# Attention with the weighted sums of two units ago laid between the scores in sixteenths, and own scores that contract over 32 rows

## What is computed

```python
q = _conv1x1(wq, x).reshape(n, NH, HD, H, W)          # n=4, NH=16 heads, HD=16, H=W=128
k = _conv1x1(wk, x).reshape(n, NH, HD, H, W)
v = _conv1x1(wv, x).reshape(n, NH, HD, H, W)
qk = jnp.einsum('nhcij,nhciw->nhijw', q, k) / D
qrq = jnp.einsum('nhcij,chjw->nhijw', q, rq) / D
krk = jnp.einsum('nhcij,chjw->nhijw', k, rk) / D
weight = jax.nn.softmax(qk + Gq * qrq + Gk * krk, axis=3)
out = jnp.einsum('nhijw,nhciw->nhcij', weight, Gv1 * v) + jnp.einsum('nhijw,chjw->nhcij', weight, Gv2 * rv)
return _conv1x1(wo, out.reshape(n, C, H, W))
```

## Time and profile before

| | us |
|---|---|
| median of 3 executions | 8304.97 |
| lowest and highest of them | 8296.95, 8308.47 |
| profiled execution: device time | 8291.75 |
| profiled execution: span from first to last instruction | 8290.0 |
| attention, from its first matmul to its last (1525.8 to 6664) | 5138.2 |
| mean granted TensorE clock, share of 2.4 GHz: whole span | 0.749 |
| the same in attention alone | 0.68 |

### The profile page before, as it was taken

How to read it: one execution, slowest core, us unless ns; L and a number is a source line. 1 busy time by engine, 2 the same in 40 slices (tenths; PEclk the granted TensorE clock), 3 DMA queues, 4 the chain that set the end, 5 groups by cost and what they waited for, 6 DMA issues and landing times. The chain is left out here.

```text
span 8290.0 us, 275612 instructions
## 1 busy us (share of the span) xinstructions
PE 7187.2 (87%) x106442; PEld 6044.4 (73%) x106442; DVE 5176.6 (62%) x20646; ACT 4856.3 (59%) x11427; POOL 2457.0 (30%) x1235
## 2 busy tenths in 40 slices
PE   4999999799999999999999899999999966766738
PEld 3555555689988888898899898898888932332338
DVE  5444444366666666666666666666666768988830
ACT  1444444577777777777777777777777733333410
POOL 0000000243443443444434444434434432322210
PEclk7999999666666666666666666666667688988855
DMA  7555555565655665655556656656656576766522
GB/s 217 203 203 204 204 204 197 113 112 100 112 103 98 113 107 101 107 99 107 101 106 112 102 100 109 109 99 110 105 100 109 92 232 203 265 201 202 208 74 99
DMA packets 1721071, 1148.11 MB, mean 138 GB/s; under 512 B 1143009, under 2 KB 1506145, under 8 KB 1703329
## 3 DMA queue, kind: packets, MB, share of 16 engines
q1 hardware_dynamic: 1530336, 842.56, 48.1%
q10 hardware_dynamic: 188352, 285.27, 9.3%
q0 software_dynamic: 1024, 2.09, 0.1%
HBM read 708.04 MB, written 421.56 MB: 136 GB/s over the span
## 5 line engine op out<-in xcount | busy, mean ns | idle before, releaser
L787 POOL TENSOR_TENSOR att_scores<-att_scores,att_inverse 128x1024 f32<-128x1024 f32 x1024 | 1966.8, 1934 | 2951.7 <-DVE att_inverse L722 2951.7
L660 ACT ACTIVATE att_scores<-att_scores,att_negmax 128x128 f32<-128x128 f32 x8192 | 2509.2, 399 | 67.6 <-issue 67.6
L737 DVE CUSTOM_DVE_ANT_0 att_scores<-att_ps,att_scores 128x128 f32<-128x128 f32 x8192 | 1780.8, 286 | 1066.7 <-PE att_ps L573 957.5
L560 PE MATMUL att_ps<-att_qk,att_rs 32*128 32x64 f32 x32768 | 1793.2, 380 | 155.6 <-ACT att_scores L652 114.2
L560 PEld LDWEIGHTS att_ps<-att_qk,att_rs 32*128 32x128 f32 x32768 | 1698.6, 299 | 196.2 <-ACT att_scores L652 142.5
L573 PE MATMUL att_ps<-att_own 16*128 16x128 f32 x16384 | 1541.6, 405 | 231.3 <-issue 224.1
L573 PEld LDWEIGHTS att_ps<-att_own 16*128 16x128 f32 x16384 | 1416.2, 300 | 268.9 <-issue 264.4
L652 ACT ACTIVATE att_scores<-att_ps 128x1024 f32<-128x1024 f32 x1024 | 992.4, 1021 | 1044.3 <-PE att_ps L560 1044.3
L720 DVE TENSOR_REDUCE att_total<-att_scores 128x8 f32<-128x1024 f32 x1024 | 1233.7, 1205 | 70.7 <-issue 70.7
L594 PE MATMUL att_ps<-att_scores,att_rv 128*16 128x64 f32 x32768 | 1249.6, 334 | 11.0 <-issue 10.8
L594 PEld LDWEIGHTS att_ps<-att_scores,att_rv 128*16 128x16 f32 x32768 | 1193.6, 127 | 24.5 <-issue 13.1
(11 more groups left out here) (146 smaller groups left out, 5276.0 us busy)
## 6 DMA issues: line engine op xcount, KB each, us to landing
qk<-proj_qk_out ACTq DMA_DIRECT2D x64, 2048.0 KB, 8.5
att_qk<-qk SPq DMA_DIRECT2D x512, 256.0 KB, 6.7
att_own<-qk SPq DMA_DIRECT2D x2048, 64.0 KB, 2.5
proj_x<-in_x_dram SPq DMA_DIRECT2D x128, 512.0 KB, 4.3
v_t<-proj_v_out ACTq DMA_DIRECT2D x64, 1024.0 KB, 11.3
att_vt<-v_t SPq DMA_DIRECT2D x128, 512.0 KB, 5.5
att_v<-att_att_v SPq DMA_DIRECT2D x512, 128.0 KB, 4.2
att_r<-att_att_r SPq DMA_DIRECT2D x512, 128.0 KB, 3.5
```

The costliest lines, as they stand in the source:

```text
L560: last = pe.matmul(ps[:, 4 + g, jj * IU:(jj + 1) * IU], rs[32 * g:32 * g + 32, t * JB + jj, :], qk[b][32 * g:32 * g + 32, :, t * JB + jj], ...
L660: last = act.activation(scores[v][:, i, :], scores[v][:, i, :], ACT.Exp, bias=negmax[v][:, i:i + 1], scale=-1.0)
L737: last = dve.tensor_tensor_reduce(out=scores[v][:, i, :], in0=ps[:, 2 * (p % 2) + r // 4, (r % 4) * W:(r % 4 + 1) * W], in1=scores[v][:, i ...
L787: pool.tensor_tensor(scores[v][:, rows, :], scores[v][:, rows, :], inverse[v][:, rows].unsqueeze(2).broadcast_to([P, PR, W]), ALU.mult).th ...
```

## The change

In `attend`, and in two sizes that `combine` reads:

- The sums are now those of **two** units ago. They are cut into quarters of fills and laid between the scores. Each quarter t of a unit holds four own pieces, relative round t and one fill each of v and rv.
- An own piece is now 4 rows of **one** group in one bank (`PR = 4`, sixteen pieces), and contracts **32** rows. The 16 rows beside the data are zeroed once at the start. VectorE's sums and GpSimd's divisions keep pieces of 8 rows (`SR`).
- PSUM: own scores have banks 0 and 1, relative scores 2 to 5, sums with v bank 6, sums with rv bank 7, each of the last two a single buffer. All v fills are copied by VectorE, all rv fills by ScalarE.
- `vt`, `att_v` and `att_r` are split into halves. Loads and stores follow half by half: 16 stores and 2 loads of v per unit. `att_r` in DRAM has blocks of 16 columns in place of 32 (`JT`), which `combine` reads.
- The halves of the next head's tables: the first is still loaded in unit k = 6, but is scaled ahead of GpSimd's piece 6 of that unit. The second is loaded in unit k = 7 and scaled ahead of piece 2 of that unit.

The core of the diff:

```diff
-PR = 8
+PR = 4
+SR = 8
-JT = JG
+JT = JG // 2
@@ own_scores
-                for r in range(4):
-                    for gg in range(2):
-                        g = 2 * (p % 2) + gg
-                        last = pe.matmul(ps[:, g, r * W:(r + 1) * W], own[half][32 * g:32 * g + HD, 1, at, :], own[half][32 * g:32 * g + HD, 0, at, :],
+                half, g = p // (PIECES // 2), p % G
+                for r in range(PR):
+                    at = (p // G) % (HROWS // 16) * PR + r
+                    last = pe.matmul(ps[:, p % 2, r * W:(r + 1) * W], own[half][32 * g:32 * g + 32, 1, at, :], own[half][32 * g:32 * g + 32, 0, at, :],
@@ unit of the tensor block
+                for t in range(FILLS):
+                    if now:
+                        own_scores(u, 4 * t)
+                    if ahead:
+                        relative(u + 1, o, t, (0, 1))
+                    if sums:
+                        sums_with_v(u - 2, b, t, (0, 1))
+                    if now:
+                        own_scores(u, 4 * t + 1)
+                    if ahead:
+                        relative(u + 1, o, t, (2,))
+                    if sums:
+                        sums_with_r(u - 2, b, t, (0,))
+                        sums_with_v(u - 2, b, t, (2, 3))
+                    if now:
+                        own_scores(u, 4 * t + 2)
+                    if ahead:
+                        relative(u + 1, o, t, (3,))
+                    if sums:
+                        sums_with_r(u - 2, b, t, (1, 2))
+                    if now:
+                        own_scores(u, 4 * t + 3)
+                    if sums:
+                        sums_with_r(u - 2, b, t, (3,))
@@ unit of the sync block
-                fresh = left >= 2 and k == UPH - 2
+                if started >= 3:
+                    store(*before(h, k, 3), u - 3, 1)
+                if k == UPH - 1 and left >= 1:
+                    load_relative(h + 1, 1)
@@ head of the gpsimd block
-                        if k == UPH - 2 and not last and p in (2, 4):
-                            scale_relative(h + 1, p // 2 - 1)
+                        if k == UPH - 2 and not last and p == 6:
+                            scale_relative(h + 1, 0)
+                        if k == UPH - 1 and not last and p == 2:
+                            scale_relative(h + 1, 1)
```

More of the change, by code:

```diff
@@ L564, in own_scores @@
             def own_scores(u, p):
-                half, block16 = p // (PIECES // 2), (p % (PIECES // 2)) // 2
+                half, g = p // (PIECES // 2), p % G
                 if p % (PIECES // 2) == 0:
@@ L640, in _ @@
+            pe.wait_ge(cleared, 3)
             for t in range(ROUNDS):
-                relative(0, 0, t)
+                relative(0, 0, t, (0, 1, 2, 3))
             units(pe, unit)
@@ new lines, in read_r, with unit @@
+            def read_r(u, b):
+                act.wait_ge(r_done, FILLS * u + b + 1)
+                if b % 2 == 0:
+                    later(act, r_stored[b // 2], 64 * u)
+                act.activation(att_r[b // 2][:, :, (b % 2) * JB:(b % 2 + 1) * JB], ps[:, 7, :].rearrange("p (j i) -> p i j", i=IU), ACT.Copy).then_inc(r_read, 1)
+            BEHIND = 2
+            def unit(u, v, now, ahead, late, sums):
+                for p in range(PIECES):
+                    if p < BEHIND:
+                        if late:
+                            exp_piece(u - 1, (v - 1) % BUFS, PIECES - BEHIND + p)
+                    elif now:
+                        exp_piece(u, v, p - BEHIND)
+                    if p % 4 == 3:
+                        if ahead:
+                            read_relative(u + 1, (v + 1) % BUFS, p // 4)
+                        if sums:
+                            read_r(u - 2, p // 4)
@@ new lines, in _, with unit @@
+            BEHIND = 2
+            def unit(u, v, now, ahead, late, sums):
+                for p in range(PIECES):
+                    if now:
+                        add_and_largest(u, v, p)
+                    if sums and p % 4 == 2:
+                        read_v(u - 2, p // 4)
+                    if p % 2 == 1:
+                        k = p // 2 - BEHIND
+                        if k >= 0 and now:
+                            sums_of(u, v, k)
+                        elif k < 0 and late:
+                            sums_of(u - 1, (v - 1) % BUFS, SPIECES + k)
@@ L773, in _ @@
+            for half in range(2):
+                dve.memset(own[half][:, :, :, :], 0.0).then_inc(cleared, 1)
+            dve.memset(ps[:, 6:8, :], 0.0).then_inc(cleared, 1)
             units(dve, unit)
```

326 lines of the change are left out of this document (122 added, 204 removed).

## The result

| | before | after |
|---|---|---|
| median of four executions, us | 8300.96 | 8834.24 |
| lowest, highest | 8291.03, 8308.47 | 8827.62, 8839.04 |
| ratio to before, with its 95% interval | | 1.0643 (1.0624 to 1.0661) |
| span of the profiled execution | 8290.0 | 8829.7 |
| attention, first matmul to last | 5138.2 | 5681.5 |

The changed kernel is 6.4% slower, against 9.0% in the forecast of 9050 us (750 us over the 8300 us of before). The time lies in attention alone. Its clock rose, and it still takes 543 us more. (The last matmul of attention before ends at 6662.6, 1.4 us ahead of the window's end, so 545 us by the matmuls.)

The account below looks back on a forecast made before the run. TensorE was taken to bound the kernel. Attention: units 5120, loop turns 226, heads 225, slow stretches 270, end 30, together 5871 us against 5138 (+733); combine +10; so 9050 us, 8-in-10 range 8400 to 11,700.

Parts of the forecast that it names:

- That the clock would be fast but for stretches: The forecast's own case for TensorE in attention: 9050 us, range 8550 to 9400, chance 0.42.
- the clock slow always: Rival for attention: TensorE's clock stays at 0.50 throughout, 62.5 us a unit, 11,640 us, chance 0.25.
- rival B: Attention: TensorE's clock is slow half of the time, 51.25 us a unit, 10,220 us, chance 0.13.
- The ordinary unit: One attention unit on TensorE at the fast clock: 22.5 + 3.5 + 9.2 + 4.8 = 40.0 us.
- the price of a change of tiling: TensorE going between row and column tiles: 0.3 us a pair (0.2 to 0.4), 16 pairs a unit, 4.8 us.
- Own pieces on one group: Row-tiled scores: one-group steps add up, 48 steps a quarter, 192 a unit, 22.5 us fast or 41.8 slow.
- Loop turn: Gaps in TensorE's issue once in four units, unchanged: 32 x 7.06 = 226 us.
- New head: TensorE waits twice for GpSimd's table scaling, about 6 and 6.5 us: 15 us a head, 225 us for 15.
- Hidden behind 40, just: SyncE's queue with its added stores and load: 32 to 37 us a unit, just hidden behind the unit's 40.
- Slow stretches: Low clock in attention: 1.5 slow quarters of 5.6 us on each loop turn, 8.4 x 32 = 270 us.
- C: Faster: clock always fast, tiling changes 0.1 us a pair, 36.8 us a unit, 8170 us, chance 0.12.
- D: Clock always fast, 0.2 us a tiling pair, 6 us a head, 38.4 us a unit, 8430 us, chance 0.08.

Follow-up runs that it names:

- x_rows16: The changed kernel with own scores contracting 16 rows again, the zero rows left out: 9977 us, ratio 1.2006 to the kernel before.
- b_rows32: The kernel before with own scores contracting 32 rows, 16 of them zeros, same order and buffers: 8245 us, ratio 0.9947.
- x_eighths: x_pair's doubled own pieces in an even order of eighths, 8 pairs of tiling changes a unit and not 12: 7936 us, ratio 0.9567 to before.
- x_pair: The changed kernel with own pieces of two neighbouring groups issued record by record in turn, into two banks: 8082 us, ratio 0.9767 to before.
- x_half_turns: The changed kernel's matmuls in a coarser order, 8 pairs of tiling changes a unit and not 16: 8402 us, ratio 1.0145 to before.
- x_early3: x_early2 with the load of one half of v issued right behind the unit's own q and k loads: 8514 us, ratio 1.0264 to before.
- x_early2: x_early with the gain loaded a unit earlier and the first half scaled ahead of GpSimd's piece 4: 8655 us, ratio 1.0449 to before.
- x_early: The changed kernel with the next head's tables scaled earlier on GpSimd and the second half's load moved ahead: 8633 us, ratio 1.0424 to before.
- x_best: x_eighths with eight units in a loop pass and the early gain load and scaling of x_early2: 7703 us, ratio 0.9286 to before.
- x_best2: x_best with the load of v moved ahead as in x_early3: 7625 us, ratio 0.9199 to before.

## Why the prediction was right, and by how much its steps missed

Of the 216 us by which the forecast was too high, 190 lie in attention, 10 in combine, 10 in the step from the profiled execution to the median (3 us after, 13 before), and the rest outside both stages.

**That the clock would be fast but for stretches** was the choice that decided, and it was made at a chance of 0.42 against 0.25 and 0.13 for the clock slow always or half of the time. It came out at 0.91. The text named the reason for it (twice the rows, sums never far), and x_rows16 and b_rows32 show it to be both of these together in this order of work. The evidence was thin. x_rows16 is rival B in the flesh: the same order at 16 rows gave a clock of 0.68 and 9977 us, where B had 10,220. That rival's price was near, and it decided on 16 rows of zeros.

**The ordinary unit** was 40.0 us, and 39.0 were measured: -128 us. The step that was mis-sized is the price of a change of tiling, 0.235 us a pair and not 0.3. This 0.235 is what is left of the quarter when the forecast's 48 steps and its sums are taken off, so these two terms are borne out together with it; that x_eighths takes 1.1 us a unit less than x_pair for four pairs less, where 0.9 would be due, is a second reading of it. The first direction had been read from one start in the trace of before (0.2 us). Why it came later there was not settled.

**Own pieces on one group** are the largest part of the loss, and x_pair shows it: the same work with two groups at once is 752 us faster, of which some 120 are its four pairs of changes fewer. The other parts are shown as well, the changes of tiling by x_half_turns (432 us, overlap included) and the new heads by x_early3 (321 us). This step above all said faster clock and slower kernel, and it is the firmest part of the prediction.

**Loop turn.** 32 turns of 7.06 us were taken, and 29 of 5.5 were measured: -66 us. The forecast had read the gaps alone as the turn's price in the kernel before, and missed the 2.4 us in the unit behind it.

**New head.** Two waits of about 6 us by GpSimd's chain were read from the order and the earlier trace rows, and both came, 6.4 us idle each. The 15 us a head that were taken left room for a later load of the second half's tables by SyncE. That did not happen in the changed kernel: 13.2 us, -27 us in all. "Hidden behind 40, just" was right for it. How little room there was came out in x_early2: with GpSimd out of the way and the table loads moved ahead, another load of the same queue, that of v, came late.

**Slow stretches** were taken at 270 us, 1.5 quarters at each turn. 287 were measured, +17 us, but not where they were put: 5.6 us and not 8.4 at each turn, and 8.3 at each head, for which nothing had been counted. The forecast had said that a head brings idle time, and then costed only the turns.

**The ends** took 44 us and not 30 (+14), as the start of the stage had been left out, and **combine** took 0 and not 10.

**Rivals C and D.** C asked for pairs at 0.1 us and D for 0.2 with a cheap head. With the measured 0.235 and x_early3's head, the kernel takes 8514 us, 84 above D's 8430. So D was near in its mechanism. What kept it from its time is the low clock behind the turns (some 145 us in x_early3, units k = 0 and 4), which it had set to nothing, and 0.6 us a unit (77 us). Its turns and heads were dearer than measured, by some 70 us each.

The Trainium skill (TensorE: Matmul & The Clock Gate, "Why this matters for your kernels") gives idle gaps between matmuls as what costs the clock. The gaps of this kernel did cost it, and the rule would have given the 287 us above their reason. It does not tell of x_rows16, where the clock fell at 4005 with TensorE busy throughout.

## What to carry to other kernels

Laying dense matmuls between sparse ones can hold TensorE's clock, but cost it per stretch: a piece of row-tiled work on one group takes its full steps in its place in the order, so issue small pieces of two or more groups record by record in turn. After such a change, a remaining wait can have two prices, its own length and the low clock behind it (in the changed kernel 4 to 6 us of time behind waits of 5 to 6 us, and by an estimate from x_early's k = 7 of 54.2 us, x_early3's of 45.4 and 2.6 us of waits a head, some 3 us behind one of about 1 us), so waits that cost little at a slow clock become the next thing to remove. With two groups at once (x_pair) the second price was gone behind a turn. And when a wait goes, look at what stands behind it in the in-order queues: here first GpSimd's scaling, then a load behind 16 us of other issues.

## What the runs showed of the hardware

- Rows of zeros count for the granted clock. 32 contracted rows in place of 16 (with equal steps, 1.09 against 1.08 us for 8 records) raised the mean clock in attention from 0.68 to 0.91 in the changed kernel's order. They gained 0.5% in the order of before, and 0.3% in the order of x_best.
- The clock fell with TensorE busy from end to end (x_rows16, 1.00 to 0.50 at 4005; x_half_turns at 4006.7), so idle time is not its only cause.
- Changing between row and column tiles cost about 0.12 us in each direction at the fast clock, as what is left of a quarter over its steps.
- Low clock behind a gap was mostly 17.1 us long in the changed kernel, whether the gap was the 3.5 + 1.7 us of a loop turn or the 6.4 us of a wait. In x_half_turns it was 10.2 us behind the heads' waits, and in x_best2 no stretch of low clock behind the start of the stage is longer than 10.2 us. Why it is shorter there was not settled.
